# The subtraction of the maximum in the first cross attention, moved from GpSimd (POOL) to VectorE

## The chip, the cores and the metric

The program runs on one core of a Trainium2 chip. The metric is the device time of one execution in microseconds. A core has a matmul engine (TensorE; the profile calls its multiplications PE and its weight loads PEld), VectorE (DVE), ScalarE (ACT), GpSimd (POOL), and SyncE (SP), which here only issues transfers. Each engine runs its own list of instructions in order; they meet only at semaphores.

## What is computed

A decoder of two layers over x of shape 2 x 2048 x 512 in float32: attention, cross attention, a feed-forward block, then a convolution block, a second cross attention and a mixture of experts. The change touches only the first cross attention, which reads a context of 77 tokens per batch, 16 heads of 32:

```python
q = split_heads(layernorm(x) @ Wq.T + bq)      # 2 x 16 x 2048 x 32
k = split_heads(ctx @ Wk.T + bk)               # 2 x 16 x 77 x 32
v = split_heads(ctx @ Wv.T + bv)
scores = einsum('bhqd,bhkd->bhqk', q / sqrt(32), k) + ((1 - mask) * -10000)[:, None]
probs = softmax(scores, axis=-1)               # max, subtract, exp, sum, divide
x = x + merge_heads(einsum('bhqk,bhkd->bhqd', probs, v))
```

## The kernel before

Each block of the network is a stage of its own, with a barrier of all engines at its end. `stage_cross` is called twice: as `xa` for the first cross attention (no output projection, so `gated` is false), and as `xb` for the second (`gated` is true). The profile names their buffers xa_... and xb_....

The 4096 rows are cut into 8 chunks of 512 rows, each into 4 tiles of 128 rows, and each tile into two halves of 8 heads. One (tile, half) is a step: 8 steps in a chunk, G = 64 in the stage. In a step the scores of 128 rows are 8 heads by 77 keys, 616 numbers per partition. They pass through these instructions, the lines being those of the profile:

- PE L1007: the scores of step g, into the first two PSUM banks. There is only one such pair of banks, so PE waits at L1002 until the mask has been added to the scores of step g-1.
- DVE L846: scores (PSUM) plus mask, into `s` in SBUF. DVE L851: the maximum of each head, into `mx`.
- POOL L801: `s` minus the maximum, in place. Before it POOL waits at L800 for the maximum.
- ACT L967: exponential, in place, after a wait at L966 for the subtraction.
- DVE L863 and L867, two steps later (LS = 2): the sum of each head and its reciprocal. POOL L797: `s` times the reciprocal, in the same step.
- PE L1016, three steps after the scores (LT = 3): the probabilities turned; ACT L952 copies them out. PE L1027, four steps after (LV = 4): times v; ACT L964 copies. PE L1039, every second step: turned back; DVE L875 adds x.

`s` has five buffers (SR = 5), `mx` two. Besides, the next chunk is prepared: in the steps u = 0 to 3 of a chunk DVE normalises one tile each (L824), which PE turns one step later (L981); PE projects the queries (L991), 8 matmuls for each of two column blocks, 16 in a row, at the end of step u = 5 and again at the end of step u = 7. In u = 7 DVE also scales the next mask (L830) and takes statistics (L811, L817). The last chunk has no next one, so none of this.

Within step g DVE works in this order: adding x (every second step), sum and reciprocal of step g-2, mask and maximum of step g, then normalising. POOL's order is: scaling step g-2, subtracting the maximum of step g. In the second stage, `xb`, DVE already subtracts the maximum (L857), and POOL only scales. There the mask is added in only 4 of the 64 steps; in the other 60 the maximum and the subtraction read the scores straight from PSUM.

Of the kernel before, what the change touches and what calls it, by code (L numbers as in the profile page):

```python
# [8 lines left out]
ALU = mybir.AluOpType  # L9
# [3 lines left out]
P = 128  # L13
# [7 lines left out]
SK = 77  # L21
# [607 lines left out]
def stage_cross(nc, tag, x_in, x_out, ident_d, ctxT_d, mask_d, wq, wk, wv, bq=None, bk=None, bv=None, wo=None):  # L629


    HB = H // 2
    U = 2 * TJ
    G = NC * U
    NT = NC * TJ
    LS, LT, LV, LO = 2, 3, 4, 8
    SR = 5
# [4 lines left out]
    gated = wo is not None  # L642
    with Stage(nc, tag) as st:
# [16 lines left out]
        s_sb = st.sb("s", [P, SR, HB, SK])  # L660
        mx = st.sb("mx", [P, 2, HB])
# [32 lines left out]
        max_done = st.sem("max_done")  # L694
        sub_done = st.sem("sub_done")
# [16 lines left out]
        masked = lambda g: not gated or (g // U) % CB == 0 and (g % U) // 2 == 0  # L712
# [62 lines left out]
        @block.gpsimd  # L775
        def _(pool):
            pool.memset(half_c[:, :], -0.5).then_inc(half_set, 1)
            pool.memset(kblk[:, :, :, :], 0.0).then_inc(zeroed, 1)
            pool.wait_ge(half_set, 1)

            def rstd(c):
                p = c % 2
                pool.wait_ge(mv_done, part(c, TJ - 1))
                if c >= 2:
                    pool.wait_ge(xn_done, part(c - 2, TJ - 1))
                pool.tensor_scalar(rs[:, p], mv[:, p, :, 1], EPS, None, ALU.add).then_inc(var_done, 1)
                pool.wait_ge(var_done, c + 1)
                pool.tensor_tensor(rs[:, p], rs[:, p], half_c[:, :], ALU.pow).then_inc(rs_done, 1)

            rstd(0)  # L790
            rstd(1)
            for g in range(G + LS):
                v = g - LS
                if v >= 0:
                    s3 = s_sb[:, v % SR]
                    pool.wait_ge(rec_done, v + 1)
                    pool.tensor_tensor(s3, s3, rec[:, v % 2].unsqueeze(2).to_broadcast([P, HB, SK]), ALU.mult).then_inc(mul_done, 1)  # L797
                if not gated and g < G:
                    s3 = s_sb[:, g % SR]
                    pool.wait_ge(max_done, g + 1)  # L800
                    pool.tensor_tensor(s3, s3, mx[:, g % 2].unsqueeze(2).to_broadcast([P, HB, SK]), ALU.subtract).then_inc(sub_done, 1)  # L801
                if g % U == U - 1 and g // U + 2 < NC:
                    rstd(g // U + 2)

        @block.vector
        def _(dve):
            def stats(c):
                p = c % 2
                dve.wait_ge(x_ld[c % XR], 16 * (c // XR + 1))
                for t in range(TJ):  # L810
                    dve.bn_stats(bn[:, p, t, :], x[:, c % XR, t, :]).then_inc(bn_done, 1)  # L811
                if c >= 2:
                    dve.wait_ge(var_done, c - 1)
                    dve.wait_ge(xn_done, part(c - 2, TJ - 1))
                for t in range(TJ):
                    dve.wait_ge(bn_done, part(c, t))
                    dve.bn_aggr(mv[:, p, t, :], bn[:, p, t, :]).then_inc(mv_done, 1)  # L817

            def normalise(c, t):
                p = c % 2  # L820
                dve.wait_ge(rs_done, c + 1)
                if c >= 2:
                    dve.wait_ge(x_mm, part(c - 2, t))
                dve.tensor_scalar(xn[:, p, t, :], x[:, c % XR, t, :], mv[:, p, t, 0:1], rs[:, p, t:t + 1],  # L824
                                  ALU.subtract, ALU.mult).then_inc(xn_done, 1)

            def ready_mask(c):
                if not gated:
                    dve.wait_ge(mask_in[c % 2], 16 * (c // 2 + 1))
                    dve.tensor_scalar(mask[:, c % 2], mask[:, c % 2], 10000.0, -10000.0, ALU.mult, ALU.add).then_inc(mask_set, 1)  # L830

            def score(g):
                c, u = g // U, g % U
                dve.wait_ge(s_mm, g + 1)
                if g >= SR:
                    dve.wait_ge(p_mm, g - SR + 1)
                s3 = s_sb[:, g % SR]
                raw = ps[:, 0:2, 0:W4].rearrange("p m (h s) -> p m h s", h=4)
                s4 = s3.rearrange("p (m h) s -> p m h s", m=2)
                if masked(g):  # L840
                    if not gated:
                        dve.wait_ge(mask_set, c + 1)
                    elif g == 0:
                        dve.wait_ge(mask_in[0], 16)
                    row = mask[:, c % 2 if not gated else 0, u // 2]
                    dve.tensor_tensor(s4, raw, row.unsqueeze(1).unsqueeze(1).to_broadcast([P, 2, 4, SK]), ALU.add).then_inc(add_done, 1)  # L846
                    dve.wait_ge(add_done, adds(g))
                if g >= 2:
                    dve.wait_ge(sub_done, g - 1)
                if masked(g):  # L850
                    dve.tensor_reduce(mx[:, g % 2], s3, AX.X, ALU.max).then_inc(max_done, 1)  # L851
                else:
                    dve.tensor_reduce(mx[:, g % 2].rearrange("p (m h) -> p m h", m=2), raw, AX.X, ALU.max).then_inc(max_done, 1)
                if gated:
                    dve.wait_ge(max_done, g + 1)
                    top = mx[:, g % 2].rearrange("p (m h) -> p m h", m=2).unsqueeze(3).to_broadcast([P, 2, 4, SK])
                    dve.tensor_tensor(s4, s4 if masked(g) else raw, top, ALU.subtract).then_inc(sub_done, 1)  # L857

            def total(g):
                dve.wait_ge(exp_done, g + 1)  # L860
                if g >= 2:
                    dve.wait_ge(rec_done, g - 1)
                dve.tensor_reduce(den[:, g % 2], s_sb[:, g % SR], AX.X, ALU.add).then_inc(den_done, 1)  # L863
                dve.wait_ge(den_done, g + 1)
                if g >= 2:
                    dve.wait_ge(mul_done, g - 1)
                dve.reciprocal(rec[:, g % 2], den[:, g % 2]).then_inc(rec_done, 1)  # L867

            def add_rows(T):
                c, t = T // TJ, T % TJ  # L870
                dve.wait_ge(o_mm, T + 1)
                if t == 0 and c >= 2:
                    dve.wait_ge(stored[c % 2], 16 * (c // 2))
                bank = 6 + wide_at["out", T] % 2
                dve.tensor_tensor(y[:, c % 2, t, :], ps[:, bank, :], x[:, c % XR, t, :], ALU.add).then_inc(y_done, 1)  # L875

            stats(0)
            for t in range(TJ):
                normalise(0, t)
            for b in range(B):  # L880
                dve.wait_ge(kv_mm, KD + b + 1)
                if biased:
                    dve.wait_ge(kv_in, 16 * loads_kv)
                    dve.tensor_tensor(v_s[:, b], ps[0:SK, 6 + b, :], bvB[:, :], ALU.add).then_inc(v_set, 1)
                else:
                    dve.tensor_copy(v_s[:, b], ps[0:SK, 6 + b, :]).then_inc(v_set, 1)
            ready_mask(0)
            stats(1)
            for g in range(G + LO + 2):
                c, u = g // U, g % U  # L890
                if g > LO and (g - 1 - LO) % 2 == 0 and (g - 1 - LO) // 2 < NT:
                    add_rows((g - 1 - LO) // 2)
                if LS <= g < G + LS:
                    total(g - LS)
                if g < G:
                    score(g)
                    if u < TJ and c + 1 < NC:
                        normalise(c + 1, u)
                if g < G and u == U - 1:
                    if c + 1 < NC:  # L900
                        ready_mask(c + 1)
                    if c + 2 < NC:
                        stats(c + 2)
# [1180 lines left out]
G = 64  # L2084
# [670 lines left out]
```

## Time and profile before

| | us |
|---|---|
| median of 3 runs | 5706.85 (5705.23 to 5709.15) |
| the profiled execution | 5697.25 |
| its span | 5695.3 |
| busy over the span: PE / DVE / ACT / POOL | 5279.1 / 2605.3 / 1695.9 / 1269.8 |
| the stretch 767 to 1100 us, about the stage `xa`: PE / DVE / ACT / POOL | 312.8 / 212.1 / 170.6 / 169.8 of 333 |

Times in the rows are microseconds from the start of the span. A row of the timeline is start, duration, engine, line, operation, output and inputs, with the number of instructions merged into it, and in brackets the time that the engine sat idle before it and what ended that.

### The profile page before, as it was taken

What the parts mean: (1) busy time and instruction counts of PE and PEld (TensorE: products, weight loads), DVE (VectorE), ACT (ScalarE), POOL (GpSimd) and SP (SyncE); (2) the same over time, 40 slices, a digit from 0 to 9 for tenths busy, and PEclk for the clock granted to TensorE, in tenths of its full rate; (3) what the DMA queues carried; (4) which work ended last, traced back from release to release, by engine and by line L of the source; (5) the groups of instructions that cost most, each with busy time, mean ns of one, the idle gap of its engine ahead of it and who ended that gap; (6) DMA issues with size and microseconds to landing.
All of it is one profiled execution on the core that took longest, in us unless ns stands there. A gap on an engine that the chain in (4) does not pass through costs nothing. (4 is left out here: it accounts for less than half of the span.)

```text
span 5695.3 us, 76040 instructions
## 1 busy us (share of the span) xinstructions
PE 5279.1 (93%) x25936; PEld 2619.1 (46%) x25936; DVE 2605.3 (46%) x4211; ACT 1695.9 (30%) x2290; POOL 1269.8 (22%) x918
## 2 busy tenths in 40 slices
PE   8999989899999899799978997569999999999999
PEld 4444446544445444344433554524444444444444
DVE  3252247554343232354532553745555455555554
ACT  1011025422211100333321442124444444444443
POOL 1010025411122000000011221423333333333333
PEclk9999999999999999999989999689999999999999
DMA  1010022310011322889875011378688745746546
GB/s 55 8 52 0 15 74 65 93 54 28 4 45 59 110 96 81 199 201 207 199 209 175 30 38 69 107 277 293 229 302 288 277 122 175 269 155 204 193 126 230
DMA packets 437257, 770.97 MB, mean 135 GB/s; under 512 B 64386, under 2 KB 207238, under 8 KB 436564
## 3 DMA queue, kind: packets, MB, share of 16 engines
q1 hardware_dynamic: 375892, 724.24, 38.8%
q0 software_dynamic: 34304, 44.13, 4.0%
q10 hardware_dynamic: 26880, 0.19, 0.3%
q8 instruction: 113, 1.85, 0.1%
q14 instruction: 68, 0.56, 0.0%
HBM read 576.17 MB, written 116.79 MB: 122 GB/s over the span
## 5 line engine op out<-in xcount | busy, mean ns | idle before, releaser
L2637 PE MATMUL ex_ps<-ex_w,ex_xT 128*64 128x512 f32 x5376 | 1228.2, 599 | 16.9 <-DVE ex_w L2521 16.7
L2521 DVE COPY ex_w<-ex_shelf 128x4096 f32 x336 | 770.3, 2293 | 520.5 <-PE ex_ps L2637 378.5
L2572 ACT ACTIVATE ex_w<-ex_shelf 128x4096 f32 x168 | 607.8, 3618 | 1044.8 <-PE ex_ps L2653 1010.5
L2637 PEld LDWEIGHTS ex_ps<-ex_w,ex_xT 128*64 128x64 f32 x5376 | 373.5, 137 | 653.8 <-issue 610.1
L2653 PE MATMUL ex_ps<-ex_w,ex_hT 128*64 128x256 f32 x5376 | 611.7, 380 | 5.5 <-ACT ex_hT L2588 3.8
L2491 POOL DMA_INDIRECT out<-ex_y,ex_ix_out x168 | 288.9, 1719 | 1177.6 <-DVE ex_ix L2509 800.9
L2653 PEld LDWEIGHTS ex_ps<-ex_w,ex_hT 128*64 128x64 f32 x5376 | 390.1, 137 | 271.0 <-issue 100.9
L2474 POOL DMA_INDIRECT ex_x<-moe_xn,ex_ix x168 | 410.1, 2441 | 97.0 <-issue 51.3
L1398 PE MATMUL ff_ps<-ff_w,ff_hT 128*128 128x512 f32 x768 | 347.8, 596 | 0.9 <-DVE ff_w L1280 0.9
L1555 PE MATMUL pr_ps<-pr_w,pr_xT 128*128 128x512 f32 x768 | 337.2, 596 | 4.7 <-DMA pr_bias<-L_attn_bq 4.7
L1353 ACT ACTIVATE ff_gT<-ff_ps,ff_bet,ff_gam 128x128 f32<-128x128 f32 x384 | 144.3, 460 | 455.7 <-PE ff_ps L1406 455.6
L2527 DVE TENSOR_TENSOR ex_h<-ex_g,ex_ps 128x512 f32<-128x512 f32 x168 | 115.4, 687 | 305.9 <-PE ex_ps L2637 289.6
L608 PE MATMUL at_ps<-at_xT,at_kT 128*128 128x512 f32 (+3 forms) x640 | 239.3, 529 | 1.6 <-ACT at_kT L505 1.6
L1420 PE MATMUL ff_ps<-ff_gT,ff_w 128*128 128x512 f32 x512 | 226.8, 596 | 0.0
L1555 PEld LDWEIGHTS pr_ps<-pr_w,pr_xT 128*128 128x128 f32 x768 | 144.7, 191 | 176.5 <-issue 176.5
L2021 POOL TENSOR_TENSOR go_xb<-go_xr,go_bias 128x2048 f32<-128x2048 f32 x8 | 38.2, 4778 | 840.0 <-DMA go_bias<-L_attn_bo 770.3
L1398 PEld LDWEIGHTS ff_ps<-ff_w,ff_hT 128*128 128x128 f32 x768 | 139.4, 192 | 141.5 <-issue 139.0
L1521 DVE TENSOR_TENSOR pr_y<-pr_ps,pr_bias 128x512 f32<-128x512 f32 x96 | 66.4, 692 | 246.6 <-PE pr_ps L1555 246.6
L1941 PE MATMUL cv_ps<-cv_y,cv_inv 64*128 64x256 f32 x1024 | 140.1, 417 | 38.4 <-DVE cv_y L1869 38.4
L608 PEld LDWEIGHTS at_ps<-at_xT,at_kT 128*128 128x128 f32 x640 | 116.7, 190 | 121.8 <-issue 109.1
L1863 DVE TENSOR_TENSOR cv_m<-cv_z,cv_hat 128x512 f32<-128x512 f32 x128 | 79.9, 686 | 201.2 <-ACT cv_z L1822 201.2
L1907 PE MATMUL cv_ps<-cv_xin,cv_split 128*128 128x512 f32 x320 | 153.5, 624 | 18.6 <-DVE cv_xin L1839 18.6
(272 smaller groups left out, 6961.5 us busy)
## 6 DMA issues: line engine op xcount, KB each, us to landing
ex_shelf<-L_ffn_w SPq DMA_DIRECT2D x128, 2048.0 KB, 16.5
ex_shelf<-L_ffn_wo SPq DMA_DIRECT2D x64, 2048.0 KB, 11.8
cv_gt<-cv_g SPq DMA_DIRECT2D x320, 128.0 KB, 3.3
cv_vt<-cv_v SPq DMA_DIRECT2D x256, 128.0 KB, 4.1
ff_x<-x SPq DMA_DIRECT2D x16, 1024.0 KB, 7.8
at_low<-x SPq DMA_DIRECT2D x8, 1024.0 KB, 5.6
x<-at_acc SPq DMA_DIRECT2D x8, 1024.0 KB, 4.2
xa_x<-x SPq DMA_DIRECT2D x8, 1024.0 KB, 7.6
```

Of the source, the lines that this page charges most:

```text
L608: i = pe.matmul(ps[:, bank + ic - origin // CH, lo - ic * CH:], kT[:, k, j * P:(j + 1) * P], xT[:, k, lo:(ic + 1) * CH], start=k == 0, sto ...
L1353: i = act.activation(gT[:, s % 2, k, j * P:(j + 1) * P], ps[:, 2 + j % 2, k * P:(k + 1) * P], ACT.Gelu, bias=bet[:, b, k:k + 1], scale=gam ...
L1398: i = pe.matmul(ps[:, j % 2, :], hT[:, k, span(s, j)], w[:, b % 2, 0, k, :], start=k == 0, stop=k == KD - 1)
L1420: i = pe.matmul(bank, w[:, b % 2, 1, k, u * P:(u + 1) * P], gT[:, s % 2, k, :], start=k == 0, stop=k == KD - 1)
L1555: i = pe.matmul(ps[:, u % 4, :], f.xT[:, p, k, (u % TJ) * P:(u % TJ + 1) * P], w[:, u // TJ, k, :], start=k == 0, stop=k == KD - 1)
L1907: i = pe.matmul(bank, split[:, u // 4, :], rows, start=True, stop=True)
L2474: pool.indirect_dma_start(out=x[:, p, :], out_offset=None, in_=xn_q, in_offset=bass.IndirectOffsetOnAxis(ap=ix[:, p:p + 1], axis=0)).then_ ...
L2491: pool.indirect_dma_start(out=out_q, out_offset=bass.IndirectOffsetOnAxis(ap=ix_out[:, p:p + 1], axis=0), in_=y[:, p, :], in_offset=None, ...
L2521: dve.tensor_copy(w_s[n][:, :], pick(shelf[n], buf)).then_inc(w_set[n].sem, 1)
L2572: act.activation(w_s[2][:, :], pick(shelf[2], buf), ACT.Copy).then_inc(w_set[2].sem, 1)
L2637: mm = pe.matmul(ps[q * G:(q + 1) * G, which, 0:FQ], xT[:, p % 2, k, :], wu[which][:, k, q * FQ:(q + 1) * FQ], start=k == 0, stop=k == KD - 1)
L2653: mm = pe.matmul(ps[q * G:(q + 1) * G, 4, 0:DQ], hT[:, p % 2, k, :], wd[:, k, q * DQ:(q + 1) * DQ], start=k == 0, stop=k == FC - 1)
```

## The change

The branch on `gated` around DVE's subtraction goes, so that `xa` too subtracts on DVE, right behind its own maximum, and POOL's subtraction is removed. `sub_done`, on which ACT and DVE wait, is now raised by DVE in both stages. Since every step of `xa` has a mask, the new DVE instruction reads `s` and `mx`, both in SBUF. The second stage stays as it was.

```diff
@@ POOL
                     pool.tensor_tensor(s3, s3, rec[:, v % 2].unsqueeze(2).to_broadcast([P, HB, SK]), ALU.mult).then_inc(mul_done, 1)
-                if not gated and g < G:
-                    s3 = s_sb[:, g % SR]
-                    pool.wait_ge(max_done, g + 1)
-                    pool.tensor_tensor(s3, s3, mx[:, g % 2].unsqueeze(2).to_broadcast([P, HB, SK]), ALU.subtract).then_inc(sub_done, 1)
@@ VectorE, score(g)
-                if gated:
-                    dve.wait_ge(max_done, g + 1)
-                    top = mx[:, g % 2].rearrange("p (m h) -> p m h", m=2).unsqueeze(3).to_broadcast([P, 2, 4, SK])
-                    dve.tensor_tensor(s4, s4 if masked(g) else raw, top, ALU.subtract).then_inc(sub_done, 1)
+                dve.wait_ge(max_done, g + 1)
+                top = mx[:, g % 2].rearrange("p (m h) -> p m h", m=2).unsqueeze(3).to_broadcast([P, 2, 4, SK])
+                dve.tensor_tensor(s4, s4 if masked(g) else raw, top, ALU.subtract).then_inc(sub_done, 1)
```

## Rows read from the trace of the kernel before

**Rows 1.** Busy time by engine in one chunk of the loop.

```profile
core 0: us, PE busy (x) PEld busy (x) DVE busy (x) ACT busy (x) POOL busy (x), PEclk, DMA share, GB/s
914.00:951.00 37.00, 36.91 (x324) 23.79 (x322) 26.68 (x49) 20.52 (x33) 21.52 (x18) 1.00 0.19 63
```

**Rows 2.** Who waited for whom, 806 to 1090 us: total, times, longest.

```profile
DVE xa_s L846 <- PE xa_ps L1007: 87.3, 15, 19.5
ACT xa_s L967 <- POOL xa_s L801: 56.0, 64, 3.2
```

**Rows 3.** Group by line, 780 to 1100 us: busy us, mean ns, idle before.

```profile
L801 POOL TENSOR_TENSOR xa_s<-xa_s,xa_mx 128x616 f32<-128x616 f32 x64 | 84.4, 1319 | 103.5 <-DVE xa_mx L851 103.1
```

**Rows 4.** Timeline of PE, one chunk: scores of u = 5, turning, projection.

```profile
928.80 0.80 PE L1007 MATMUL xa_ps<-xa_kblk,xa_qT 64*128 64x154 f32 x8
...
929.52 1.10 PE L1016 MATMUL xa_ps<-xa_ident,xa_s 128*77 128x128 f32 x8
...
931.13 7.13 PE L991 MATMUL xa_ps<-xa_xT,xa_wq 128*128 128x512 f32 x16
```

**Rows 5.** Timeline of DVE in the same chunk, from u = 0 to u = 6.

```profile
914.33 0.80 DVE L846 TENSOR_TENSOR xa_s<-xa_ps,xa_mask 128x616 f32<-128x616 f32 x1 [3.16 <-PE xa_ps L1007]
...
915.88 0.54 DVE L824 TENSOR_SCALAR xa_xn<-xa_x,xa_mv,xa_rs 128x512 f32<-128x512 f32 x1
...
916.51 0.69 DVE L875 TENSOR_TENSOR xa_y<-xa_ps,xa_x 128x512 f32<-128x512 f32 x1
...
922.52 0.54 DVE L824 TENSOR_SCALAR xa_xn<-xa_x,xa_mv,xa_rs 128x512 f32<-128x512 f32 x1
...
922.97 0.68 DVE L875 TENSOR_TENSOR xa_y<-xa_ps,xa_x 128x512 f32<-128x512 f32 x1
...
927.44 0.79 DVE L846 TENSOR_TENSOR xa_s<-xa_ps,xa_mask 128x616 f32<-128x616 f32 x1
...
928.27 0.80 DVE L851 TENSOR_REDUCE xa_mx<-xa_s 128x8 f32<-128x616 f32 x1
...
928.98 0.68 DVE L875 TENSOR_TENSOR xa_y<-xa_ps,xa_x 128x512 f32<-128x512 f32 x1
...
939.03 0.80 DVE L846 TENSOR_TENSOR xa_s<-xa_ps,xa_mask 128x616 f32<-128x616 f32 x1 [5.97 <-PE xa_ps L1007]
```

**Rows 6.** Timeline of POOL in the same chunk.

```profile
926.21 1.45 POOL L801 TENSOR_TENSOR xa_s<-xa_s,xa_mx 128x616 f32<-128x616 f32 x1 [0.32 <-DVE xa_mx L851]
...
927.62 1.21 POOL L797 TENSOR_TENSOR xa_s<-xa_s,xa_rec 128x616 f32<-128x616 f32 x1
...
929.14 1.22 POOL L801 TENSOR_TENSOR xa_s<-xa_s,xa_mx 128x616 f32<-128x616 f32 x1 [0.31 <-DVE xa_mx L851]
```

**Rows 7.** Timeline of DVE in the second cross attention, a step with a mask.

```profile
3328.64 0.80 DVE L851 TENSOR_REDUCE xb_mx<-xb_s 128x8 f32<-128x616 f32 x1
3329.47 0.80 DVE L857 TENSOR_TENSOR xb_s<-xb_s,xb_mx 128x616 f32<-128x616 f32 x1
3330.19 0.54 DVE L824 TENSOR_SCALAR xb_xn<-xb_x,xb_mv,xb_rs 128x512 f32<-128x512 f32 x1
```

**Rows 8.** Timeline of the first chunk: mask of u = 4, scores of u = 5.

```profile
817.09 0.76 DVE L846 TENSOR_TENSOR xa_s<-xa_ps,xa_mask 128x616 f32<-128x616 f32 x1
...
818.22 0.80 PE L1007 MATMUL xa_ps<-xa_kblk,xa_qT 64*128 64x154 f32 x8
```

**Rows 9.** Timeline of the last chunk, from u = 0 to u = 7.

```profile
1063.22 0.80 DVE L851 TENSOR_REDUCE xa_mx<-xa_s 128x8 f32<-128x616 f32 x1
...
1064.56 0.69 DVE L875 TENSOR_TENSOR xa_y<-xa_ps,xa_x 128x512 f32<-128x512 f32 x1 [0.55 <-PE xa_ps L1039]
...
1066.11 0.79 DVE L846 TENSOR_TENSOR xa_s<-xa_ps,xa_mask 128x616 f32<-128x616 f32 x1
...
1067.04 0.80 PE L1007 MATMUL xa_ps<-xa_kblk,xa_qT 64*128 64x154 f32 x8 [0.19 <-DVE xa_s L846]
...
1082.73 0.79 DVE L846 TENSOR_TENSOR xa_s<-xa_ps,xa_mask 128x616 f32<-128x616 f32 x1
```

## The prediction

> **What bounds the kernel now.** The change lies inside one stage of some 330 us, between two barriers, so I read that stage alone. First its chunks by engine [rows 1]: in a chunk of 37 us PE is busy for 36.9 us, DVE for 26.7, POOL for 21.5. PE looks like the bound, with 10.3 us of DVE left over. Then the waits [rows 2]: DVE waits for PE's scores 15 times, 87.3 us in all, the first of them 19.5 us, before the loop. The other 14 are two for each of the first seven chunks, and the timeline shows where: 5.97 us before the mask of step u = 6 and 3.16 us before that of u = 0 [rows 5], that is, while PE does its 16 projection matmuls of 7.13 us each time [rows 4]. Between the mask of u = 0 at 914.33 and u = 6 DVE has no such wait. So DVE's spare time isn't spread over the chunk: it lies behind the two projections, and in the six steps from u = 0 to u = 5 both DVE and PE are full. The reader should see these two faces of one chunk.
>
> What couples them is a single pair of PSUM banks for the scores: PE may compute step g+1 only once DVE has added the mask of step g. DVE can't run late by a step and make it up in the projection. How tight it is can be read at the end of the six steps: the mask of u = 4 ends at 927.44 + 0.79 = 928.23 [rows 5], PE's scores of u = 5 start at 928.80 [rows 4]. Where PE does wait for the mask, it starts 0.14 us behind its end (1066.11 + 0.79 = 1066.90, then 1067.04) [rows 9]. So PE has 928.80 - 928.23 - 0.14 = 0.43 us of slack there.
>
> **The change, part by part.** POOL loses 64 subtractions of 1319 ns, 84.4 us [rows 3]. None of that is on the path: DVE never waits for POOL, and PE is full. ACT's exponential did wait for it, 56.0 us over 64 times [rows 2], but its result is wanted by DVE only two steps later; this gain is worth 0 as long as that cover of two steps holds, and the change shortens the chain, so it does. POOL's own queue then holds only scalings and the small statistics, no later than before.
>
> DVE gains 64 subtractions and as many waits for its own maximum. Queued behind each of them on DVE are normalising, adding x and, two steps on, the sum and reciprocal, and then the next mask, for which PE waits. The cost of one: the same instruction with both inputs in SBUF stands in the second cross attention, in its masked steps: maximum to subtraction 3329.47 - 3328.64 = 0.83, subtraction to the next instruction 3330.19 - 3329.47 = 0.72 [rows 7], together 1.55. Today the maximum is followed by the next instruction after 928.98 - 928.27 = 0.71 [rows 5]. So each step becomes longer by d = 1.55 - 0.71 = 0.84 us. The lower bound is a subtraction that hides the latency between maximum and subtraction wholly, 0.72; the upper bound is below.
>
> Now which of the 64 are on the path.
> - Chunks 1 to 6 (six of them). Ahead of the mask of u = 4 stand the four subtractions of u = 0 to 3: 4 x 0.84 = 3.36. Two reserves are used up first: in u = 0 DVE comes to adding x 0.63 us after normalising (915.88 to 916.51), where elsewhere it takes 0.45 (922.52 to 922.97) [rows 5], since it waits 0.18 for PE; and PE's 0.43. Delay of the projection: 3.36 - 0.18 - 0.43 = 2.75 us. The subtraction of u = 4 delays only the mask of u = 5, whose result PE wants after the projection, 7 us on. Those of u = 5 and 6 fit into the 5.97 us of waiting, that of u = 7 into the 3.16. So four in eight cost, and the chunk grows by 2.75: 6 x 2.75 = 16.5.
> - The first chunk. The mask of u = 4 ends at 817.09 + 0.76 = 817.85, the scores of u = 5 start at 818.22 [rows 8]: slack 0.23 us, and no adding of x yet. 3.36 - 0.23 = 3.1.
> - The last chunk has no projections. DVE paces it from u = 0 to 7. Its only reserve is the wait of adding x in u = 0: 1064.56 - 1063.22 = 1.34 where 0.71 is usual, 0.63 [rows 9]. The mask of u = 7 (1082.73) comes 7 x 0.84 - 0.63 = 5.25 later. The eighth subtraction comes before the exponential that POOL's subtraction fed; it is shorter than that was, and the sum after it is covered by PE's and ACT's last steps. 5.3.
> Sum: 16.5 + 3.1 + 5.3 = 24.9 us. The stage ends in a barrier, so the whole of it passes on. Two edits that I put at nothing: POOL's scaling comes directly when the reciprocal is done, earlier by some tenths, hidden since PE takes it a step later; and POOL's subtraction took 1.45 us where it met DVE's normalising and 1.22 where it didn't [rows 6], a quarrel that goes away, on an engine that was not waited for. If DVE was slowed by it as well, by the 0.03 us that separates its 0.76 [rows 8] from its 0.79 us [rows 5] for the same mask, that gives back some 0.06 a step, 2 us over the 35 steps on the path.
>
> In the profiled execution that is 5697.25 + 24.9 = 5722.2. The median of the runs is 9.6 us above that execution, so I take 5706.85 + 24.9 = 5731.8, say 5732.
>
> **A rule to weigh.** The new subtraction starts 0.83 + 0.83 = 1.66 us behind the start of its step's mask. POOL's scaling starts 0.18 us behind that same start (927.62 against 927.44) and ends at 0.18 + 1.21 = 1.39 [rows 5, 6]. So the two miss each other by 0.27 us in every step. The Trainium skill, "SBUF — State Buffer", section "Who interferes with whom", says that a VectorE instruction with two SBUF inputs contends with a GpSimd instruction that reads SBUF, and that whichever starts second is fully blocked. This speaks against the change, since the new instruction has two SBUF inputs and the scaling reads SBUF; by that rule the sum stays as it is while the two miss each other, and becomes that of the second rival if they don't. No row of this trace shows the pair overlapping.
>
> **The rivals.**
> 1. DVE's idle time takes it all: same as before. 8 x 0.84 = 6.7 us a chunk is less than the 5.97 + 3.16 = 9.1 us in which DVE waits for PE [rows 5]. It would be so if DVE might lag behind PE by more than a step. It decides at 4d - 0.18 = 0.43, that is, for a d under 0.15 us; against it stands d = 0.84 [rows 7] and the single pair of banks. Time 5707. The shorter chain to the exponential can add a gain only where PE waits for ACT, at the stage's two ends, about 1 us each; then 5705.
> 2. Scaling and subtraction collide. If POOL's scaling had to begin behind the subtraction, it would start at 1.66 + 0.80 = 2.46 instead of 0.18: 2.3 us later. PE wants the scaled scores one step on: today at 929.52 [rows 4], 0.69 us after 927.62 + 1.21 = 928.83 [rows 6]. After the change the scaling is 4 x 0.84 - 0.18 = 3.18 us later there and PE 2.75, which leaves 0.26. So 2.3 - 0.26 = 2.0 us more in each of seven chunks, 14 in all: 24.9 + 14 = 39, time 5746. Against it: the 0.27 us of distance.
> 3. Every subtraction is exposed, since DVE's waits behind the projections turn out to be needed by something I took as covered: 64 x 0.84 = 53.8, time 5761. Against it: 5.97 and 3.16 us are far above 0.84.
> 4. With PE waiting in the narrow steps its granted clock falls. It is 1.00 (2.4 GHz) now with PE at 99% [rows 1]; PE would be at 93% after. The six steps hold 931.13 - 914.33 = 16.8 us of PE's work a chunk [rows 4, 5]; at 1.2 GHz twice that, over 100 us in all.
>
> **How the numbers follow.** About 0.2%, 11.4 us, is what a measurement of this kernel can tell from no change. Forecast (delay of 18 to 32 us) 0.79. Rival 1: 0.09, most of it same. Rival 2: 0.06. Rival 3: 0.04. Rival 4: 0.02. The lower end: d = 0.72 over the 35 subtractions on the path takes 4.2 off, DVE relieved of POOL takes 2 off, runs spread by 2 to 4: 5706.85 + 24.9 - 4.2 - 2 - 4 = 5721.5. The upper end is rival 2 with the spread of the runs, 5746 + 3 = 5749. That range leaves out rivals 1, 3 and 4, 0.15. Slower 0.90, within 0.2% 0.07, faster 0.03.
>
> **What would show it.** Right: in a chunk after, a period of 37.0 + 2.7 = 39.7 us; PE idle before the scores of u = 2 to 5, released by DVE's mask, about 2.7 us a chunk; DVE's wait behind the first projection down to 5.97 + 2.75 - (6 x 0.84 - 0.18) = 3.9 us, behind the second to about 2.1; steps of the last chunk longer by 0.84 each; the subtraction at 0.80 us on DVE; POOL's scaling at 1.22. Wrong: a scaling of 1.45 us or more that starts or ends with the subtraction (rival 2), PE waiting for POOL, a granted clock under 1.00 between 840 and 1100 us, or a delay of the stages behind the barrier that isn't the stage's own.

## The result, and the profile after

The changed kernel takes 5734.89 us in the median (5732.36 to 5744.15) against 5705.62 of before: 1.0054 times, 95% interval 1.0039 to 1.0069, or 22 to 39 us more. The profiled execution took 5732.36 us, its span 5730.2. Run a second time, beside other runs of before, it came to 5729.84 against 5701.70, 1.0045 (1.0028 to 1.0062).

The loop of the stage, from the start of its first mask to the start of the last adding of x, can be cut at the masks of VectorE (L846 before, L842 after). All in us, from the timelines:

| | first chunk | chunks 1 to 6 | last chunk, up to the mask of u = 7 | from there to the last adding of x | loop |
|---|---|---|---|---|---|
| before | 33.95 | 222.07 | 20.35 | 11.72 | 288.1 |
| after | 36.95 | 238.60 | 25.57 | 11.77 | 312.9 |
| difference | 3.00 | 16.53 | 5.22 | 0.05 | 24.8 |
| forecast | 3.1 | 16.5 | 5.25 | 0 | 24.9 |

The same chunk as [rows 1] is now 39.8 us long, with PE busy for 37.7 of them, DVE for 32.9 and POOL for 11.0. Busy time of each engine in it:

```profile
core 0: us, PE busy (x) PEld busy (x) DVE busy (x) ACT busy (x) POOL busy (x), PEclk, DMA share, GB/s
925.80:965.60 39.80, 37.69 (x321) 23.86 (x322) 32.94 (x58) 20.43 (x32) 10.97 (x10) 1.00 0.18 58
```

The timeline of DVE over that chunk, rows that answer to [rows 5], with the mask of u = 0 of this chunk and of the next at the ends (start, duration; in brackets the idle time before and what ended it):

```profile
925.82 0.80 DVE L842 TENSOR_TENSOR xa_s<-xa_ps,xa_mask 128x616 f32<-128x616 f32 x1 [2.13 <-PE xa_ps L1002]
...
942.10 0.79 DVE L842 TENSOR_TENSOR xa_s<-xa_ps,xa_mask 128x616 f32<-128x616 f32 x1
...
942.92 0.80 DVE L847 TENSOR_REDUCE xa_mx<-xa_s 128x8 f32<-128x616 f32 x1
...
943.75 0.80 DVE L852 TENSOR_TENSOR xa_s<-xa_s,xa_mx 128x616 f32<-128x616 f32 x1
...
944.47 0.68 DVE L870 TENSOR_TENSOR xa_y<-xa_ps,xa_x 128x512 f32<-128x512 f32 x1
...
953.28 0.80 DVE L842 TENSOR_TENSOR xa_s<-xa_ps,xa_mask 128x616 f32<-128x616 f32 x1 [3.88 <-PE xa_ps L1002]
...
965.59 0.80 DVE L842 TENSOR_TENSOR xa_s<-xa_ps,xa_mask 128x616 f32<-128x616 f32 x1 [2.13 <-PE xa_ps L1002]
```

Maximum to the next instruction of the old order is now 944.47 - 942.92 = 1.55 us, where it was 0.71. The waits behind the projections have shrunk from 5.97 to 3.88 and from 3.16 to 2.13 [rows 5]: the subtractions of u = 5 to 7 lie there and cost nothing.

The timeline of PE, rows that answer to [rows 4], with the scores of u = 4 ahead of them:

```profile
939.26 0.80 PE L1002 MATMUL xa_ps<-xa_kblk,xa_qT 64*128 64x154 f32 x8 [1.10 <-DVE xa_s L842]
...
941.30 0.66 PE L976 MATMUL xa_ps<-xa_ident,xa_xn 128*128 128x128 f32 x4 [0.21 <-DVE xa_xn L820]
...
943.04 0.80 PE L1002 MATMUL xa_ps<-xa_kblk,xa_qT 64*128 64x154 f32 x8
...
945.37 7.13 PE L986 MATMUL xa_ps<-xa_xT,xa_wq 128*128 128x512 f32 x16
```

PE now stands still for 1.10 us before the scores, until DVE has added the mask of the step before. The scores of u = 5 (943.04) come 0.15 us behind the end of the mask of u = 4 (942.10 + 0.79 = 942.89), with no idle time of their own: PE's turning of the normalised tile, which waits for DVE too, brings it to the same moment. Over the loop, PE's waits for VectorE (for its mask ahead of the scores, L1007 before and L1002 after, and for a normalised tile, L981 and L976) have grown, and it now waits twice for POOL, both times behind the last mask. Total, times and longest, first before, then after:

```profile
PE xa_ps L1007 <- DVE xa_s L846: 2.5, 4, 1.0
PE xa_ps L981 <- DVE xa_xn L824: 0.4, 1, 0.4
```

```profile
PE xa_ps L1002 <- DVE xa_s L842: 15.1, 20, 1.5
PE xa_ps L976 <- DVE xa_xn L820: 6.1, 20, 1.2
PE xa_ps L1011 <- POOL xa_s L797: 1.9, 2, 1.0
```

POOL's scaling in this step keeps its distance, and its length:

```profile
942.26 1.22 POOL L797 TENSOR_TENSOR xa_s<-xa_s,xa_rec 128x616 f32<-128x616 f32 x1 [2.55 <-DVE xa_rec L862]
```

It ends at 943.48, 0.27 us before the subtraction starts at 943.75. In both profiles of the changed kernel all 64 subtractions take 0.80 us and all 64 scalings 1.21 or 1.22.

One thing did change that the table doesn't show. TensorE's granted clock, 1.00 (2.4 GHz) through the whole loop before, falls in the first chunk after PE has waited 0.99 and 1.23 us for VectorE there (columns as in the window above):

```profile
814.00:821.00 7.00, 5.26 (x26) 4.25 (x26) 6.83 (x12) 2.82 (x4) 2.37 (x2) 0.51 0.00 0
```

VectorE is busy for 6.83 of these 7 us and waits for nothing, so the low level, close to 0.50 (1.2 GHz), costs no time.

### The profile page after: what moved, and what is told of

It reads as the page before. It is cut to its first block and busy times, and to the rows that moved or that the text cites. A ratio compares the mean times of both kernels' runs of the same rounds, so it can differ in the third digit from the quotient of the medians.

```text
span 5730.2 us, 76040 instructions
## 1 busy us (share of the span) xinstructions
PE 5290.5 (92%) x25936; PEld 2625.7 (46%) x25936; DVE 2659.4 (46%) x4275; ACT 1695.4 (30%) x2290; POOL 1187.6 (21%) x854
## 3 DMA queue, kind: packets, MB, share of 16 engines
q8 instruction: 113, 1.85, 0.1%
## 6 DMA issues: line engine op xcount, KB each, us to landing
ex_shelf<-L_ffn_w SPq DMA_DIRECT2D x128, 2048.0 KB, 16.5
```

## The experiments

The theory from the forecast, called position theory: what costs is only a subtraction that stands on VectorE ahead of the mask of u = 4 (or, in the last chunk, ahead of any mask), because PE can run one step ahead and no more. Its rival, the share theory, charges each moved subtraction alike. A second question is the price of a collision between POOL and VectorE, which the changed kernel misses by 0.27 us.

**Only the late half of each chunk.** POOL and VectorE each raise a semaphore of their own; ScalarE and VectorE wait for the one that belongs to the step (those lines are left out here).

```diff
+        on_dve = lambda g: gated or g % U >= 4
...
@@ POOL
-                if not gated and g < G:
+                if g < G and not on_dve(g):
...
@@ VectorE
-                if gated:
+                if on_dve(g):
...
```

> VectorE subtracts the maximum only in the steps u = 4 to 7 of each chunk, POOL in u = 0 to 3: 32 of the 64 subtractions are moved. Position theory (only subtractions that stand ahead of the mask of u = 4 cost, because PE may run one step ahead and no more): chunks 0 to 6 keep their periods of before (34.0 and 37.0 us), the last chunk becomes 3 x 0.84 = 2.5 us longer, the loop of the stage grows by 2.5 us from 288.0. Share theory (cost follows the amount of work moved): half of the 24.9 us, 12.4.

The chunks 0 to 6 took 33.95 and 37.01 to 37.02 us, those of before to the hundredth; the masks of u = 0 of one chunk and of the next:

```profile
914.84 0.80 DVE L849 TENSOR_TENSOR xa_s<-xa_ps,xa_mask 128x616 f32<-128x616 f32 x1 [2.13 <-PE xa_ps L1010]
...
951.85 0.80 DVE L849 TENSOR_TENSOR xa_s<-xa_ps,xa_mask 128x616 f32<-128x616 f32 x1 [2.13 <-PE xa_ps L1010]
```

The last chunk took 22.87, which is 2.52 more. The position theory holds, the share theory falls. But the loop grew by 6.4, not by 2.5: the piece behind the last mask took 15.60 us instead of 11.72. The windows of that kernel show why:

```profile
core 0: us, PE busy (x) PEld busy (x) DVE busy (x) ACT busy (x) POOL busy (x), PEclk, DMA share, GB/s
1080.00:1085.00 5.00, 4.68 (x65) 3.55 (x62) 4.86 (x9) 2.57 (x5) 1.22 (x1) 1.00 0.01 3
1085.00:1090.00 5.00, 2.99 (x36) 2.20 (x28) 4.03 (x7) 2.87 (x5) 1.97 (x2) 0.83 0.55 210
1090.00:1095.00 5.00, 4.65 (x32) 3.53 (x31) 1.59 (x3) 1.79 (x3) 1.68 (x2) 0.50 0.00 0
```

and in its timeline of PE the wait after which the clock fell, and eight matmuls of the same kind at half speed, 1.99 us for 1.10:

```profile
1087.21 1.10 PE L1019 MATMUL xa_ps<-xa_ident,xa_s 128*77 128x128 f32 x8 [2.01 <-POOL xa_s L800]
...
1090.52 1.99 PE L1019 MATMUL xa_ps<-xa_ident,xa_s 128*77 128x128 f32 x8 [0.16 <-POOL xa_s L800]
```

PE had waited 2.01 us for POOL's scaling; the granted clock went from 1.00 to 0.50 (1.2 GHz), and this time it fell where PE set the pace. The total, 5715.16 against 5702.78 (1.0020, 1.0010 to 1.0029), is 12 us more, of which the loop explains 6.4.

**Only the early half.** The same with `g % U < 4`.

> The other half: VectorE subtracts only in u = 0 to 3, POOL in u = 4 to 7. Position theory: chunks 1 to 6 have the full 39.8 us of the changed kernel, the first grows by 3.0, the last by 4 x 0.84 - 0.63 = 2.7: the loop grows by 3.0 + 16.5 + 2.7 = 22.2 us. Share theory: 12.4 again.

First chunk 36.95 (+3.00), chunks 1 to 6 238.96 in all (+16.9; five of them 39.76 or 39.77, one 40.12), the last one 23.06 (+2.71), the rest 11.72: the loop grew by 22.6. One chunk of it:

```profile
926.32 0.80 DVE L849 TENSOR_TENSOR xa_s<-xa_ps,xa_mask 128x616 f32<-128x616 f32 x1 [3.16 <-PE xa_ps L1010]
...
966.09 0.80 DVE L849 TENSOR_TENSOR xa_s<-xa_ps,xa_mask 128x616 f32<-128x616 f32 x1 [3.16 <-PE xa_ps L1010]
```

In total 5734.03, 1.0055 (1.0038 to 1.0072). Thirty-two subtractions here cost 22.6 us, the other thirty-two 2.5 and a slow clock. In u = 0 to 3 the steps are 4.38, 3.76, 4.37 and 3.77 us long, within 0.01 us of those of the changed kernel.

In the chunks 0 to 6 the steps u = 0 to 3 are also those with normalising. That this isn't the reason is shown by the last chunk, which has none: three subtractions of its late half cost 2.52 us, four of its early half 2.71, that is 4 x 0.84 less the reserve of 0.63.

**Late half, last chunk left alone.** `g % U >= 4 and g < G - U`.

> VectorE subtracts the maximum only in u = 4 to 7 of chunks 0 to 6 (28 of 64 subtractions), POOL everywhere else, the whole last chunk included. Position theory: nothing on the path, loop 288.0 us, time within 0.1% of before. Share theory: 28/64 of 24.9 = 10.9 us. It also tells whether the 4 us that the last steps of the late half lost, at a granted clock of 0.5, belong to the moved subtractions of the last chunk: then they are gone here.

33.95, then 222.08, then 20.35 and 11.71: loop 288.1 us, with 28 subtractions moved to VectorE. They are free where they stand. DVE's wait behind the first projection is 4.29 us instead of 5.97 (start, duration, idle before):

```profile
942.03 0.80 DVE L849 TENSOR_TENSOR xa_s<-xa_ps,xa_mask 128x616 f32<-128x616 f32 x1 [4.29 <-PE xa_ps L1010]
942.86 0.80 DVE L854 TENSOR_REDUCE xa_mx<-xa_s 128x8 f32<-128x616 f32 x1
943.69 0.80 DVE L860 TENSOR_TENSOR xa_s<-xa_s,xa_mx 128x616 f32<-128x616 f32 x1
```

The slow clock is gone with the moved subtractions of the last chunk. The median isn't quite that of before, 5711.18 against 5701.70 (1.0013, 1.0004 to 1.0023), though the loop of the profiled execution is; the control below bears on that, and doesn't settle it.

**One more instruction, POOL's kept.** On the kernel before, a VectorE instruction of the same size behind the maximum, on buffers that are filled once ahead of the loop and that nothing else uses, once with two SBUF inputs and once with one:

```diff
...
+                if not gated:
+                    dve.wait_ge(extra_set, 2)
+                    dve.tensor_tensor(extra[:, 1], extra[:, 0], small[:, 0].unsqueeze(2).to_broadcast([P, HB, SK]), ALU.subtract)
```

```diff
...
+                    dve.tensor_reduce(small[:, 1], extra[:, 0], AX.X, ALU.max)
```

> The kernel before, POOL's subtraction kept, with one more VectorE instruction of the same size right behind the maximum in each step of the first cross attention: it subtracts a small buffer from a large one, both in SBUF, result unused. It has no wait for the maximum, so it costs 0.71 + 0.72 - 0.71 = 0.72 us a step. If only VectorE's time counts: chunk period 37.0 + 4 x 0.72 - 0.61 = 39.3, last chunk + 7 x 0.72 - 0.63 = 4.4. It starts ahead of POOL's subtraction and overlaps it. If two SBUF inputs lock POOL out until it ends, POOL's subtraction lasts about 1.22 + 0.6 = 1.85 us in place of 1.22 to 1.45, without a change in the period beyond some 0.5 us; if they don't, it stays at 1.22 to 1.45.

> As the one before, but the extra VectorE instruction has a single SBUF input: the maximum of an unused buffer. VectorE's time only: chunk period 39.3 again. POOL's subtraction should then not be stretched by it. Normalising now starts while POOL's subtraction is under way (0.71 + 0.72 = 1.43 us behind the maximum, POOL from 0.88 to 2.10): if whichever starts second is blocked wholly, normalising lasts about 1.2 us in place of 0.54 and the period becomes 39.3 + 4 x 0.67 = 42.0; if not, normalising stays at 0.54.

The last chunk, which has no normalising, came out as forecast: 24.68 and 24.62 us, 4.3 more than before (4.4 expected); the steps of DVE are longer by 0.71, its own time and nothing else. The chunks 1 to 6 did not: with two inputs 42.85 us in three of them and 43.2 to 43.4 in the other three, with one input 40.90, where VectorE's time alone gives 37.01 + 4 x 0.71 - 0.43 - 0.18 = 39.2. Each kernel was run once: 5749.46 us, with a loop of 339.2, and 5735.88, with one of 323.7. First the extra with two inputs, DVE and POOL from the timeline:

```profile
950.33 0.79 DVE L861 TENSOR_TENSOR xa_extra<-xa_extra,xa_small 128x616 f32<-128x616 f32 x1
...
950.50 1.70 POOL L806 TENSOR_TENSOR xa_s<-xa_s,xa_mx 128x616 f32<-128x616 f32 x1 [0.32 <-DVE xa_mx L856]
951.04 1.44 DVE L829 TENSOR_SCALAR xa_xn<-xa_x,xa_mv,xa_rs 128x512 f32<-128x512 f32 x1
```

then the one with a single input:

```profile
935.09 0.78 DVE L861 TENSOR_REDUCE xa_small<-xa_extra 128x8 f32<-128x616 f32 x1
935.26 1.22 POOL L806 TENSOR_TENSOR xa_s<-xa_s,xa_mx 128x616 f32<-128x616 f32 x1 [0.32 <-DVE xa_mx L856]
935.79 0.96 DVE L829 TENSOR_SCALAR xa_xn<-xa_x,xa_mv,xa_rs 128x512 f32<-128x512 f32 x1
```

With two inputs POOL's subtraction is held up, 1.70 us instead of 1.22 (1.85 expected); with one it isn't: 1.22 in all 64. And normalising, which starts while POOL's subtraction runs, is held up in turn: 1.44 and 0.96 us instead of 0.54. I had expected 1.2 of it for the instruction with one input, and nothing for the one with two; that the two delays chain, the second instruction of VectorE paying for the first's block on POOL, was not in my sum. Four delays of 0.42 a chunk make the 1.7 us between 39.2 and 40.9, and four of 0.90 the 3.6 between 39.2 and 42.85. The three longer chunks are those in which the granted clock fell for 3.5 us; no other chunk of that kernel between the second and the last has such a stretch.

**A forced collision.** The changed kernel, with POOL's scaling held back until the maximum of the step:

```diff
...
                     pool.wait_ge(rec_done, v + 1)
+                    if not gated and g < G:
+                        pool.wait_ge(max_done, g + 1)
```

> The changed kernel, with POOL's scaling of step g-2 held back until the maximum of step g is known, so that it is released 0.05 us behind the start of VectorE's new subtraction (which has two SBUF inputs). Lock theory (second rival of the prediction): the scaling is stretched from 1.22 to about 1.9 to 2.0 us, ends 2.3 us later than before behind the mask, and the chunk period grows from 39.8 to about 41.8. Without a lock: scaling 1.22, period 41.1 (only the later start). In the last chunk the steps stay at 3.31 and 3.91 us, paced by VectorE, in both cases, unless normalising-free steps show the subtraction itself stretched.

```profile
925.18 0.80 DVE L854 TENSOR_TENSOR xa_s<-xa_s,xa_mx 128x616 f32<-128x616 f32 x1
925.29 1.76 POOL L799 TENSOR_TENSOR xa_s<-xa_s,xa_rec 128x616 f32<-128x616 f32 x1 [2.90 <-DVE xa_mx L849]
...
927.11 1.10 PE L1013 MATMUL xa_ps<-xa_ident,xa_s 128*77 128x128 f32 x8 [0.80 <-POOL xa_s L799]
```

The scaling takes 1.76 us (1.9 to 2.0 expected), PE waits for it ahead of the projection, and normalising takes 1.44 in u = 0 to 3, but for the first two steps of the loop. So the two do block each other, but my price was far too low: the periods are 46.1 to 46.2 us in five of the chunks, 50.7 in one and 42.15 in the first, not 41.8; the last chunk took 26.73 instead of 25.57, where I had expected no change; and the loop is 365.7 us, 365.7 - 312.9 = 52.8 more than that of the changed kernel. In the one execution the kernel took 5784.95 us.

The steps of one chunk tell the parts of its growth apart. Those of u = 0 to 3 are 5.28, 4.66, 5.26 and 4.67 us long, 0.9 each more than in the changed kernel, which is normalising: 3.6 us. The steps with the projections, u = 5 and 7, are 9.18 each for 7.28 and 8.39, 1.90 and 0.79 more. PE waits for the later scaling ahead of them: in u = 4, then ahead of the first projection, and ahead of the second.

```profile
968.50 1.10 PE L1013 MATMUL xa_ps<-xa_ident,xa_s 128*77 128x128 f32 x8 [0.61 <-POOL xa_s L799]
...
973.17 1.10 PE L1013 MATMUL xa_ps<-xa_ident,xa_s 128*77 128x128 f32 x8 [1.24 <-POOL xa_s L799]
...
986.27 1.10 PE L1013 MATMUL xa_ps<-xa_ident,xa_s 128*77 128x128 f32 x8 [0.72 <-POOL xa_s L799]
```

That is 3.6 + 1.9 + 0.8 = 6.3 us, the period of this chunk being 46.06. The granted clock fell in every chunk of this kernel, for 3.5 to 14 us. The five ordinary chunks differ by only 0.14 us between 3.5 and 10.3 us of it; the chunk of 50.7 us is the one in which it lasted for 13.8 us and into the first projection.

**The subtraction put off.** The changed kernel, with the subtraction of step g behind the mask of step g+1, and the exponential one step later on ScalarE. It was meant as an improvement.

```diff
...
+                    if not gated and g % U:
+                        take_off(g - 1)
                     dve.wait_ge(add_done, adds(g))
...
+                    if not gated and u == U - 1:
+                        take_off(g)
...
-                if g < G:
-                    act.wait_ge(sub_done, g + 1)
+                e = g if gated else g - 1
+                if 0 <= e < G:
+                    act.wait_ge(sub_done, e + 1)
...
```

`take_off(g)` is the subtraction of step g with its wait for the maximum.

> The changed kernel with VectorE's subtraction of step g put behind the mask of step g+1 (that of u = 7 stays in its step), and the exponential one step later on ScalarE. Position theory: the wait for the maximum vanishes from VectorE, a subtraction costs 0.61 us instead of 0.84, and only three stand ahead of the mask of u = 4: chunk period 37.0 + 3 x 0.61 - 0.61 = 38.2, first chunk + 1.6, last + 6 x 0.61 - 0.63 = 3.0 up to the mask of u = 7; the loop grows by about 12.5 us where the changed kernel grew by 24.9. If the number of subtractions ahead of the projection doesn't matter, it stays near 24.9; if the later exponential becomes the new wait, the period rises above 39.8.

It got worse: four of the chunks 1 to 6 of 40.4 us and two of 41.3 and 41.4 (in these the granted clock fell for 3.5 us), loop 324.8, in all 5741.78 (1.0070, 1.0054 to 1.0087). I had the number of subtractions right and overlooked that behind the mask they fall right into POOL's scaling. The timeline of POOL and DVE:

```profile
930.91 1.22 POOL L797 TENSOR_TENSOR xa_s<-xa_s,xa_rec 128x616 f32<-128x616 f32 x1 [3.38 <-DVE xa_rec L871]
...
931.46 1.33 DVE L861 TENSOR_TENSOR xa_s<-xa_s,xa_mx 128x616 f32<-128x616 f32 x1
```

This time POOL was first, and the subtraction takes 1.33 us instead of 0.80 (1.33 or 1.36 in 48 of the 64). Part of the growth is also a new wait of VectorE's sum for the later exponential (0.39 us, idle time ended by ScalarE), in u = 1.

**Normalising between maximum and subtraction.** The same work, with the wait for the maximum covered:

```diff
+                if not gated and g % U < TJ and g // U + 1 < NC:
+                    normalise(g // U + 1, g % U)
                 dve.wait_ge(max_done, g + 1)
```

> The changed kernel with normalising put between the maximum and the subtraction in u = 0 to 3, so that the subtraction's wait for the maximum has passed. Of the 0.84 us a step, 0.12 is that wait (0.83 between maximum and subtraction where 0.71 is usual). Position theory: four of them ahead of the projection, chunk period 39.76 - 4 x 0.12 = 39.3, last chunk unchanged at 25.57; the loop grows by 24.9 - 7 x 0.48 = 21.5 us over that of before.

```profile
929.39 0.80 DVE L847 TENSOR_REDUCE xa_mx<-xa_s 128x8 f32<-128x616 f32 x1
...
930.11 0.54 DVE L820 TENSOR_SCALAR xa_xn<-xa_x,xa_mv,xa_rs 128x512 f32<-128x512 f32 x1
930.56 0.79 DVE L854 TENSOR_TENSOR xa_s<-xa_s,xa_mx 128x616 f32<-128x616 f32 x1
931.27 0.79 DVE L860 TENSOR_REDUCE xa_den<-xa_s 128x8 f32<-128x616 f32 x1
```

Maximum to sum 1.88 us instead of 2.00 (931.02 to 933.02 in the changed kernel), periods 36.43 and 39.25 us, 0.52 shorter each: as expected (39.3). The last chunk is unchanged at 25.57. The loop gained only 0.7 all the same, since behind the last mask the granted clock fell again and that piece took 14.71 us instead of 11.77. The one execution took 5735.03 us.

**Controls.** The changed kernel and the kernel before, once more each:

> The changed kernel once more. The loop of the stage 24.9 us longer than before, as in its first profile, since the periods are set by instruction durations; all that goes beyond (10 us of 35 in that profile, 4 of 29 in the medians) differs from execution to execution in stages that the change doesn't touch, and comes out otherwise here. If the change slowed the later stages, they would be longer again by 7 us.

> The kernel before, once more, as a control for the stages outside the change. If its first profile was a lucky execution, its time to the first mask of the loop (806.4 us then, 806.9 to 810.7 in all the others) and its later stages come out some microseconds longer here too, at an unchanged loop of 288.0 us, and the ratio is 1.000. If the other programs really run slower outside the loop, this one repeats 806.4 us and the later stages of the first profile.

The changed kernel's loop was 312.9 us again, its clock low in the same two places. The kernel before had 288.1 in the loop and a span of 5703.5, 8.2 us more than in the execution of the rows above, all of it outside: 809.0 us to the first mask instead of 806.4, and 126.0 instead of 121.9 from the first to the last weight load of the turning in the routing stage (L208), for instance. Its ratio to before is 1.0002 (0.9992 to 1.0011). So the profile of before on which I worked was of a quick execution, and 10 of the 35 us between the two first spans have nothing to do with the loop. The two second profiles differ by 5726.5 - 5703.5 = 23.0 us in span and by 24.8 in the loop: outside it the changed kernel was no slower there.

## Why the prediction was right

**The bound and its two faces.** That DVE's spare time lies behind the projections and can't be used by the steps ahead of them is shown by the two halves: the early one costs 22.6 us, the late one 2.5 of VectorE's time, and nothing where the last chunk is left out. That it is the single pair of PSUM banks that couples the two rests on the program and on PE's waits for the mask, 2.5 us before and 15.1 after; no kernel with a second pair was run.

**The price of one.** 0.84 us a step, taken from the second cross attention, where the same instruction stands behind the same maximum. Measured: 1.55 - 0.71, to the hundredth. The first steps of a chunk grew from 3.73, 2.93, 3.52 and 2.93 us to 4.38, 3.77, 4.36 and 3.77, by 0.65 for the first (0.84 less the wait of 0.18 for PE) and by 0.84 for the others.

**The reserves.** Period 39.76 against 37.01: 2.75, as summed, with PE's slack of 0.43 and DVE's 0.18 used up. The wait behind the first projection is 3.88 where I gave 3.9, behind the second 2.13 for 2.1. The first chunk grew by 3.00 us for 3.1: there PE had another 0.13 us in hand between the start of the scores of u = 5 and that of the projection (2.46 us before, 2.33 after), which I hadn't counted. One sign came out otherwise: I gave PE 2.7 us a chunk of waiting before the scores of u = 2 to 5. It waits there for 0.40 (u = 2) and 1.10 (u = 4), and for 0.61 before three turnings of normalised tiles, 2.11 in all. It is VectorE that holds it up in both places.

**The gains I put at nothing** were nothing: scaling earlier, no more quarrel with POOL. The relief of 0.03 us an instruction that I allowed for in the range did not show, and its reason was wrong: the mask took 0.76 us in u = 2 to 4 of the first chunk and 0.79 or 0.80 elsewhere with POOL's subtraction and without it. PE waiting for POOL, a sign of being wrong, did occur, for 0.84 and 1.05 us behind the last mask; that piece grew by 0.05 us only.

**The rivals.** Absorbed: fell, by the halves. Collision: didn't happen in the changed kernel, at a distance of 0.27 us that held in the profile; it happens where I forced it, and there my price of 2.0 us a chunk was a third of the 6.3 measured: I had charged the delay of the first projection by the scaling alone (1.90 measured), and neither that of the second (0.79) nor the normalising that the scaling holds up in turn (3.6). Had the two overlapped, the time would have been beyond my range. All exposed: fell. The clock: it fell in the changed kernel too, for 6.9 us in the first chunk, as shown above, and for 3.5 us in the last:

```profile
1103.00:1106.00 3.00, 1.82 (x10) 1.54 (x11) 2.90 (x6) 0.98 (x3) 1.21 (x1) 0.70 0.00 0
1106.00:1109.00 3.00, 3.00 (x32) 2.31 (x32) 2.90 (x6) 1.64 (x3) 1.22 (x1) 0.73 0.00 0
```

but DVE is busy for 2.90 of 3 us there and sets the pace, so the half speed of PE cost nothing; in chunks 1 to 6 the clock stayed at 1.00. I had treated the clock as a matter of the whole loop or of nothing. In six of the kernels (the late half, the two with one more instruction, the forced collision, the subtraction put off and the one with normalising between) it fell behind the last mask, where PE sets the pace, and that piece took 14.71 to 15.60 us; in the six profiles without such a fall there it took 11.71 to 11.77.

**What is left.** The medians differ by 29.3 us, and by 28.1 the second time, where the loop gives 24.8. The rest of some 4 us lies within both intervals. The free version, too, is 9.5 us slower in the median with a loop of 288.1, at an interval whose lower end is 2 us. Whether these programs run a little slower outside the loop, or the clock falls in the last steps of some executions that weren't profiled, stays open; in the second pair of profiles the loop accounts for the whole difference.

## What to carry to other kernels

An engine that idles for a quarter of a loop may still have nothing to spare where the new work stands. Look for the point at which the other engine waits, here the single pair of PSUM banks, and count only the instructions ahead of it and the slack at that point; take the price of one from the same instruction elsewhere in the program, start to start. Where VectorE and POOL both read SBUF, write down at which moment of the step each starts, before moving anything: 0.27 us apart cost nothing, overlapping, with the scaling held back for it, cost 6.3 us in a period of 40.

## What the runs showed of the hardware

- VectorE and POOL hold each other up, in both orders. POOL's 1.22 us became 1.70 and 1.76 when it started 0.11 to 0.17 us behind a VectorE instruction with two SBUF inputs, and stayed at 1.22 behind one with one input (the maximum of a buffer). VectorE's subtraction of 0.80 became 1.33 when it started 0.55 us behind POOL's scaling; normalising, 0.54, became 0.96 and 1.44 when it started 0.53 and 0.54 us behind POOL's start. For the pairs with two SBUF inputs the traces agree with the rule of the Trainium skill, "SBUF — State Buffer", section "Who interferes with whom", that I had weighed: the one that starts second pays. Normalising has one large SBUF input, so the rule as I had weighed it doesn't cover it; it is held up all the same, and holds POOL up when it is first (1.45 us for 1.22 [rows 6]). In the recorded times the second one ends sooner than by its full duration behind the end of the first: POOL's 1.70 us ended 1.08 behind the end of VectorE's instruction, where it takes 1.22 alone, and normalising ended at 936.75, 0.27 behind POOL's end at 936.48, where it takes 0.54. Whether part of its work was done meanwhile, or part of its time needs no SBUF, isn't shown.
- The delays chain: an instruction of VectorE that blocks POOL makes POOL block the next one of VectorE for longer (normalising 1.44 us behind the extra instruction with two inputs, 0.96 behind the one with one).
- Waiting for the result of the instruction just before it costs VectorE 0.12 us (0.83 us from start to start, 0.71 without), and an independent instruction in between takes that back: 0.52 us in a chunk with four.
- TensorE's granted clock fell to 0.50 (1.2 GHz) for 3.5 to 14 us at a time in loops in which PE waits a little in most steps, and came back. Where VectorE set the pace it cost nothing (6.9 us in the first chunk of the changed kernel, 3.5 in its last); where PE did, the piece behind the last mask grew by 2.9 to 3.9 us, and two chunks of the kernel with the subtraction put off were 0.9 us longer than their neighbours.
